# Routed tokens in 39 units of 128 rows (16 blocks of two, 7 of one) in place of 23 blocks of 256, with two raw weight buffers

## What is computed

```python
x = x + _layernorm(_L0_attn_ref(_layernorm(x), Wq, Wk, Wv, Wo, b_out))
x = x + _layernorm(_L0_ffn_ref(_layernorm(x), w_router, wg, wu, wd, sg, su, sd))

# _L0_ffn_ref: E = 8, TOPK = 2, H = 256, I = 640, NSH = 2
scores = sigmoid(xt @ w_router.T)
topk_w, topk_i = top_k(scores, 2)            # weights divided by their sum -> comb
gate = silu(einsum('th,eih->tei', xt, wg)); up = einsum('th,eih->tei', xt, wu)
out = einsum('te,teh->th', comb, einsum('tei,ehi->teh', gate * up, wd))
out = out + the same gate/up/down with sg, su, sd for the 2 shared experts, no weights
```

## Time and profile before

| what | value |
|---|---|
| median of 3 runs | 746.38 us |
| lowest, highest run | 740.99, 746.75 us |
| the profiled execution's own time | 747.06 us |
| its span, first to last instruction | 745.2 us |
| PE busy | 699.8 us, 94% of the span |
| PE weight loads busy | 556.5 us, 75% |
| DVE busy | 593.2 us, 80% |
| ACT busy | 435.8 us, 58% |
| POOL busy | 309.9 us, 42% |
| moved by DMA | 74.29 MB, mean 100 GB/s |

### The profile page before, as it was taken

The page is one execution under the profiler, slowest core; times in us unless marked ns, Lnnn a source line. Parts: engine busy times, 40 slices in busy tenths (PEclk is TensorE's granted clock), DMA queues, the critical chain, the costliest instruction groups (busy, mean ns, idle before and its releaser), DMA issues.

```text
span 745.2 us, 15380 instructions
## 1 busy us (share of the span) xinstructions
PE 699.8 (94%) x5954; PEld 556.5 (75%) x5954; DVE 593.2 (80%) x1251; ACT 435.8 (58%) x745; POOL 309.9 (42%) x445
## 2 busy tenths in 40 slices
PE   3888999999999988999999999999999999978994
PEld 2444555555555545888889999999999999867884
DVE  4999999999998884487777888888888888428885
ACT  2456766677766685442266776777777777412321
POOL 4124344444444463100264444544544531075764
PEclk9899999999999999999999999999999999998998
DMA  8000000000000000000356667667666676031211
GB/s 283 1 4 3 4 3 17 10 10 12 9 11 17 11 12 13 15 8 1 106 157 222 227 215 238 222 217 243 211 220 245 210 223 216 29 99 43 84 59 56
DMA packets 28552, 74.29 MB, mean 100 GB/s; under 512 B 4032, under 2 KB 17728, under 8 KB 28480
## 3 DMA queue, kind: packets, MB, share of 16 engines
q0 software_dynamic: 12208, 55.45, 22.9%
q1 hardware_dynamic: 15856, 17.20, 6.8%
q10 hardware_dynamic: 416, 0.66, 0.3%
HBM read 62.68 MB, written 10.22 MB: 98 GB/s over the span
## 4 chain that ended last, share of the span: by engine, by line
PE 77%; DVE 15%; issue 3%; ACT 2%; POOL 1%; DMA 1%; POOLq 0%; DVEq 0%
PE PS L438 73%; DVE NM L874 4%; DVE NM L870 3%; PE PS L449 2%; PE PS L623 1%; DVE QC L839 1%; PE PS L541 1%; DVE RR L834 1%; DVE X L1133 1%; DVE RT L846 1%; POOL RS L1221 1%; ACT PF L744 1%; DMA X<-in_x 1%; DVE KC L844 1%; DVE CTX L906 0%
## 5 line engine op out<-in xcount | busy, mean ns | idle before, releaser
L1068 DVE TENSOR_TENSOR HF<-SS,PS 128x256 f32<-128x256 f32 (+1 forms) x155 | 75.9, 490 | 95.2 <-ACT SS L787 54.1
L787 ACT ACTIVATE SS<-PS 128x256 f32<-128x256 f32 (+1 forms) x155 | 68.1, 439 | 120.1 <-PE PS L438 105.8
L438 PE MATMUL PS<-XGH,WH 128*128 128x256 f32 x460 | 129.2, 281 | 0.0
L438 PE MATMUL PS<-XGL,WH 128*128 128x256 f32 x460 | 128.9, 280 | 0.0
L438 PE MATMUL PS<-XGH,WL 128*128 128x256 f32 x460 | 128.8, 280 | 0.0
L1156 DVE TENSOR_TENSOR WL<-RAW,WH 128x768 fp32r<-128x768 f32 x125 | 119.9, 961 | 1.3 <-ACT WH L707 1.3
L438 PE MATMUL PS<-WH,HH 128*128 128x256 f32 x390 | 112.5, 289 | 7.3 <-issue 7.2
L1254 POOL TENSOR_SCALAR_AFFINE_SELECT PF<-PF 128x512 f32<-128x512 f32 x128 | 78.8, 640 | 96.8 <-ACT PF L744 96.7
L707 ACT ACTIVATE HH<-HF 128x256 fp32r<-128x256 f32 (+1 forms) x155 | 72.1, 465 | 68.9 <-DVE HF L1068 61.7
L438 PE MATMUL PS<-WL,HH 128*128 128x256 f32 x390 | 110.7, 284 | 0.0
L744 ACT ACTIVATE PF<-PS 128x1536 f32<-128x1536 f32 x64 | 92.8, 1450 | 30.6 <-PE PS L438 30.0
(11 more groups left out here) (174 smaller groups left out, 1465.7 us busy)
## 6 DMA issues: line engine op xcount, KB each, us to landing
ys<-YO SPq DMA_DIRECT2D x23, 256.0 KB
RAW<-in_wsh SPq DMA_DIRECT2D x4, 768.0 KB, 6.4
X<-in_x SPq DMA_DIRECT2D x8, 256.0 KB, 5.2
xn<-YY SPq DMA_DIRECT2D x16, 128.0 KB, 1.7
out<-X SPq DMA_DIRECT2D x16, 128.0 KB
RAW<-in_wsh SPq DMA_DIRECT2D x2, 384.0 KB, 6.2
XG<-xn,XIDX POOLq DMA_INDIRECT x46
QT<-NMT SPq DMA_DIRECT2D x32, 12.0 KB
```

The costliest lines, as they stand in the source:

```text
L438: return eng.matmul(o, l, r, start=start, stop=stop, skip_group_check=True)
L787: t = eng.activation(SS[:, i % 2, 0:n], bank(b, 0, n), ACT.Silu)
L1068: eng.tensor_tensor(HF[:, c % 2, 0:n], SS[:, c % 2, 0:n], bank(b, 512 - n, 512) if n == 256 else bank(b), ALU.mult).then_inc(free[b], 1)
```

## The change

The routed tokens lie in units of 128 slots. SUB = (4096 + 8*127) // 128 = 39 of them suffice for any routing. 16 pairs form wide blocks of 256 as before; 7 single ones are narrow blocks of 128 tokens. The number of blocks, NK, is again 23, and they run in the order W N W W N W W W N W W N W W N W W W N W W N W (W wide, N narrow), so that of UNITS. An expert whose last 256 holds at most 128 tokens puts them in a narrow one.

A narrow block has 3 chunks (2, 2 and 1 times 128 inner columns) and 121 + 20 = 141 chunks are left in all. In its `up` the tokens (XGH, XGL: 128x128) are stationary and the weights (WH, WL) move, 512 columns a matmul for a chunk of two and 256 for the last: 6 matmuls a chunk. The products HF then have tokens on the partitions, so a stage `cross` on PE transposes them (1 matmul a 128 columns) into bank 6 or 7; `hh` and `hl` of a narrow chunk read that bank and come after `cross`, one step later than for a wide chunk. `down` has 3 matmuls of 256 columns per 128 inner columns. `turn_block` has 2 transposes.

`splits()` lists at which chunk each piece is split: some 20,000 columns of matmul ahead of its use and after the last reader of its WH buffer is in the plan. In a wide block ahead of a narrow one this gives chunks with 2, 2, 1, 1 and 1 pieces; in a narrow one 1 a chunk; the five pieces of the second shared expert all stand in one chunk, the first (c = 116) of the last wide block. There are two raw buffers, RAW0 and RAW1 (the second lies where attention's small tiles were); weights are asked for two blocks ahead. The shared expert's second weights go to RAW0 and wait for the pieces of block 23, which are split in chunks 111 to 115.

`choose` 4 to 8 and 13 work on counts in 256s and in 128s: `places()` has 13 operations where 3 stood, and 5 and 13 have 1 and 2 more. The arrays over SUB shrink from 46 to 39. The weights' layout in memory is changed to match (gate and up side by side for each half of 256).

```diff
@@ -18,12 +18,20 @@
 NE = 8
 IC = 5
 TG = 4
-BLK = 256
-NK = (2 * NT * P + NE * (BLK - 1)) // BLK
-SUB = 2 * NK
+SUB = (2 * NT * P + NE * (P - 1)) // P
+WIDE = (SUB - NE + 1) // 2
+SLIM = SUB - 2 * WIDE
+UNITS = [u for _, u in sorted([((2 * k + 1) / (2 * WIDE), (2 * k, 2)) for k in range(WIDE)] +
+                              [((2 * j + 1) / (2 * SLIM), (2 * WIDE + j, 1)) for j in range(SLIM)])]
+NK = len(UNITS)
 DENSE = TG * IC
-LAST = DENSE + IC * NK
-NC = LAST + DENSE
+CHUNKS = [(0, c % IC, 1) for c in range(DENSE)]
+for k in range(NK):
+    CHUNKS += [(k + 1, m, 1) for m in range(IC)] if UNITS[k][1] == 2 else [(k + 1, 0, 2), (k + 1, 2, 2), (k + 1, 4, 1)]
+LAST = len(CHUNKS)
+CHUNKS += [(NK + 1, c % IC, 1) for c in range(DENSE)]
+NC = len(CHUNKS)
+AHEAD = 20000
...
+def wide_of(c):
+
+    return 128 * CHUNKS[c][2] if narrow(c) else 256 if DENSE <= c < LAST else 512
...
+def user(q, m):
+
+    return max(c for c in range(NC) if CHUNKS[c][0] == q and CHUNKS[c][1] <= m < CHUNKS[c][1] + CHUNKS[c][2])
+
+
+def splits():
+
+    at, first = [0], {}
+    for c in range(LAST + 1):
+        at.append(at[-1] + (4608 if not narrow(c) else 2432 * CHUNKS[c][2]))
+        for m in range(CHUNKS[c][1], CHUNKS[c][1] + CHUNKS[c][2]):
+            first.setdefault((CHUNKS[c][0], m), c)
+    out, c = {}, 0
+    for q in range(1, NK + 2):
+        for m in range(IC):
+            use = first.get((q, m), LAST + m)
+            w = max([n for n in range(min(use, LAST)) if at[n] <= at[min(use, LAST)] - AHEAD] + [DENSE - 2])
+            if q == 1:
+                w = DENSE - 2 if m < 2 else DENSE - 1
+            c = max(c, w, user(q - 2, m) + 1 if q > 1 else 0)
+            out.setdefault(c, []).append((q, m))
+    return out
...
+            if narrow(c - 1):
+                out.append(("cross", c - 1))
+                out.append(("hh", c - 1))
             out.append(("hl", c - 1))
-        q, m = sequence(c), c % IC
-        if c < DENSE:
-            pieces = {18: (0, 1), 19: (2, 3, 4)}.get(c, ())
-        else:
-            pieces = (m,) if c < LAST else ()
-        out.extend(("split", q + 1, m) for m in pieces)
-        if c < NC:
+        out.extend(("split", q, m) for q, m in pieces.get(c, ()))
+        if c < NC and not narrow(c):
             out.append(("hh", c))
...
-        elif s[0] in ("xt", "rank", "token"):
-            b = {"rank": 6, "token": 7}.get(s[0], 6 + s[1] % 2)
+        elif s[0] in ("rank", "token", "xt", "cross"):
+            b = 6 + crossed % 2
+            crossed += 1
...
-        RAW = sb("RAW", [P, 3840], F32)
+        RAW0 = sb("RAW0", [P, 3840], F32)
...
+        RAW1 = sb("RAW1", [P, 3840], F32)
+        sb("rest", [P, 320], F32)
...
+        def raw_of(q):
+
+            return 0 if q > NK else (q + 1) % 2 if q else 0
...
+                if narrow(c):
+                    o = bank(b, 0, 256 * n)
                     k6 = 0
                     for k in range(2):
-                        at = 768 * ic + 256 * m + 128 * k
-                        if block:
+                        xh = XGH[:, (q - 1) % 2, 128 * k:128 * k + 128]
+                        xl = XGL[:, (q - 1) % 2, 128 * k:128 * k + 128]
+                        wh, wl = (w[:, 768 * ic:768 * (ic + n)].rearrange("p (i c) -> p i c", c=768)[:, :, 256 * k:256 * k + 256]
+                                  for w in (hi, lo))
+                        for l, r in ((xh, wh), (xl, wh), (xh, wl)):
+                            t = mm(o.rearrange("p (i c) -> p i c", c=256), l, r, k6 == 0, k6 == 5)
+                            k6 += 1
...
+            def cross(c):
+
+                mixed(e, c)
+                b = take(("cross", c))
+                for i in range(CHUNKS[c][2]):
+                    t = eng.transpose(bank(b, 128 * i, 128 * i + 128), HF[:, c % 2, 128 * i:128 * i + 128], identf)
+                t.then_inc(full[b], 1)
...
-                        e.wait_ge(d_raw[m // 2], 16 * q)
+                        e.wait_ge(d_raw[q % 2][m // 2], 16 * ((q + q % 2) // 2))
...
-                        e.wait_ge(dn, DENSE + IC * (q - 3) + m + 1)
-                    copy(WH[q % 2][:, 768 * m:768 * m + 768], RAW[:, 768 * m:768 * m + 768]).then_inc(w_hi, 1)
+                        e.wait_ge(dn, user(q - 2, m) + 1)
+                    copy(WH[q % 2][:, 768 * m:768 * m + 768], RAW[raw_of(q)][:, 768 * m:768 * m + 768]).then_inc(w_hi, 1)
...
+                    if narrow(i):
+                        made(e, ("cross", i))
+                        copy(HH[:, i % 4, 0:n], bank(use["cross", i][0], 0, n)).then_inc(h_hi, 1)
+                    else:
+                        mixed(e, i)
+                        copy(HH[:, i % 4, 0:n], HF[:, i % 2, 0:n]).then_inc(h_hi, 1)
...
+            def places():
+
+                te = "p (t e) -> p t e"
+                c, n = use["rank", 0]
+                rank = bank(c, 0, 128).rearrange(te, e=8)
+                eng.scalar_tensor_tensor(out=CUM[:, :, :], in0=BASE[:, :, :], scalar=1.0 / 256, in1=NBK[:, :, :], op0=ALU.mult, op1=ALU.add).then_inc(lay, 1)
+                eng.tensor_scalar(BACK1[:, 0, :], NBK[:, 0, :], 256.0, None, ALU.mult, ALU.bypass)
+                eng.tensor_scalar(BACK1[:, 1, :], BASE[:, 1, :], 0.5, None, ALU.mult, ALU.bypass).then_inc(lay, 1)
+                eng.tensor_tensor(SL[:, :, :], rank, BASE[:, 0, :].unsqueeze(1).broadcast_to([P, NT, NE]), ALU.add)
+                e.wait_ge(lay, 3)
+                eng.tensor_scalar(FST[:, 0:1], CUM[:, 0, 7:8], 2.0, float(SUB - NE), ALU.mult, ALU.max).then_inc(lay, 1)
+                eng.tensor_tensor(EQ[:, :, :], rank, BACK1[:, 0, :].unsqueeze(1).broadcast_to([P, NT, NE]), ALU.is_ge).then_inc(free[c], 1)
+                eng.scalar_tensor_tensor(out=BACK1[:, 2, :], in0=CUM[:, 0, :], scalar=-256.0, in1=BACK1[:, 1, :], op0=ALU.mult, op1=ALU.add).then_inc(lay, 1)
+                e.wait_ge(lay, 4)
+                eng.tensor_scalar(FST[:, 1:2], FST[:, 0:1], 128.0, None, ALU.mult, ALU.bypass).then_inc(lay, 1)
+                e.wait_ge(lay, 6)
+                eng.tensor_scalar(CUM[:, 1, :], CUM[:, 1, :], FST[:, 0:1], None, ALU.add, ALU.bypass)
+                eng.tensor_scalar(BACK1[:, 1, :], BACK1[:, 2, :], FST[:, 1:2], None, ALU.add, ALU.bypass).then_inc(lay, 1)
+                e.wait_ge(lay, 7)
+                e.wait_ge(free[c], n)
+                eng.tensor_tensor(EQ[:, :, :], EQ[:, :, :], BACK1[:, 1, :].unsqueeze(1).broadcast_to([P, NT, NE]), ALU.mult).then_inc(lay, 1)
+                e.wait_ge(lay, 8)
+                eng.tensor_tensor(SL[:, :, :], SL[:, :, :], EQ[:, :, :], ALU.add).then_inc(lay, 1)
+                e.wait_ge(lay, 9)
+                eng.tensor_tensor(SL[:, :, :], SL[:, :, :], SG[:, 2, :].rearrange(te, e=8), ALU.mult).then_inc(rt, 1)
...
+                    eng.scalar_tensor_tensor(out=EB[:, 0, :], in0=EB[:, 0, :], scalar=NE - 0.5, in1=EB[:, 0, :], op0=ALU.is_lt, op1=ALU.mult).then_inc(rs_, 1)
                     e.wait_ge(rs_, 4)
-                    t = eng.tensor_scalar(WIDX[:, :], EB[:, :], pcol, None, ALU.add, ALU.bypass)
+                    eng.tensor_tensor(EB[:, 0, :], EB[:, 0, :], EB[:, 1, :], ALU.add).then_inc(rs_, 1)
+                    e.wait_ge(rs_, 5)
+                    eng.tensor_scalar(EB[:, 0, :], EB[:, 0, :], float(NE - 1), float(P), ALU.min, ALU.mult).then_inc(rs_, 1)
+                    e.wait_ge(rs_, 6)
+                    t = eng.tensor_scalar(WIDX[:, :], EB[:, 0, :], pcol, None, ALU.add, ALU.bypass)
...
+                    if narrow(i):
+                        c = use["cross", i][0]
+                        eng.tensor_tensor(HL[:, i % 4, 0:n], bank(c, 0, n), HH[:, i % 4, 0:n].bitcast(F32), ALU.subtract).then_inc(free[c], 1)
+                    else:
+                        eng.tensor_tensor(HL[:, i % 4, 0:n], HF[:, i % 2, 0:n], HH[:, i % 4, 0:n].bitcast(F32), ALU.subtract).then_inc(h_lo, 1)
...
             def weights(q, k):
                 lo, hi = PIECES[k]
                 e.wait_ge(w_idx, 1)
-                e.wait_ge(w_lo, IC * (q - 1) + hi)
-                eng.indirect_dma_start(RAW[:, 768 * lo:768 * hi], None, (wa, wb, wc)[k],
-                                       bass.IndirectOffsetOnAxis(ap=WIDX[:, q - 1:q], axis=0)).then_inc(d_raw[k], 16)
+                if q == 2:
+                    made(e, ("token", 0))
+                else:
+                    e.wait_ge(w_lo, IC * (q - 2 if q > 2 else 0) + hi)
+                eng.indirect_dma_start(RAW[raw_of(q)][:, 768 * lo:768 * hi], None, (wa, wb, wc)[k],
+                                       bass.IndirectOffsetOnAxis(ap=WIDX[:, q - 1:q], axis=0)).then_inc(d_raw[q % 2][k], 16)
...
+                    for k in range(3):
+                        weights(2, k)
+                elif what == "split" and 0 < i < NK - 1 and s[2] in (1, 3, 4):
+                    weights(i + 2, s[2] // 2)
...
                     if q:
-                        e.wait_ge(w_lo, IC * (q - 1) + hi)
```

(40 more changed lines are left out.)

228 lines of the change are left out of this document (122 added, 106 removed).

## The result

The changed kernel takes 721.14 us (median of 4 runs, 718.19 to 722.65), the kernel before 745.44 in as many runs beside it (740.99 to 746.75). The ratio is 0.9679, with a 95% interval of 0.9627 to 0.9732: 24.3 us, or 3.2%, faster, 2.6 us over the forecast of 718.5. The profiled execution took 720.56 with a span of 718.8.

What follows compares the result with a forecast made beforehand. PE's matmul columns were taken to bound the routed stage. From the profiled 747.06 us, minus 35.3, plus 2.8 (XGL), 3.8 (hand-over) and 0.9 (routing) gave 719.3, stated as 718.5 against the median; range 711 to 734.

Steps and rivals of the forecast that it cites:

- The gain: Routed stage: 7 narrow blocks of 6.05 us replace wide ones of 11.09, removing PE columns worth 35.3 us.
- The wait for XGL: Each narrow block: PE waits 0.4 us for XGL before the next block's first up; 2.8 us in all (0 to 7).
- The hand-over: Chunk 116, last shared expert: its late weight load, one split counted after landing, delays PE's down; loss 3.8 us (2.6 to 5.0).
- Routing: Longer places() and choose make DVE 2.7 us later at chunk 14's HF; 0.9 us lost (bounds 0 and 2.7).
- The doubled splits: Wide blocks ahead of narrow ones: DVE's two splits a chunk just fit; nothing added, upper bound 0.3 for each of 7.
- Summed up: Routed stage: DVE's total work is 195 us of 220, so PE stays the bound with 11% over it, not 18%.
- One thing stays as it is: Last stage, untouched by the change: PE's unexplained 6.90 us wait at 666 us was taken to remain.
- the second rival: Whole kernel comes out lower, at 712 us, as the hand-over is hidden or the 6.90 us pause falls away; chance 0.12.
- The first: Rival, narrow blocks: DVE paces them at 8.3 us each, 13 us more, giving 732; chance 0.15.
- The third: Rival, narrow blocks: turning gate products puts the stages in a row, 16.7 us a block, giving 786; chance 0.05.
- the fourth: Rival, routed stage: loads set the pace at 219 GB/s, needing 253 us; total 750, no change; chance 0.04.
- wrong signs: PE idle for HL or HF in narrow blocks, WH waiting for RAW, clock under 1.00 after transposes, no hand-over wait.

Runs made afterwards that it cites:

- experiment 1: Changed kernel with all 23 blocks wide and none narrow, everything else of the change kept: 739.21 us, ratio 1.0005 to the kernel before.
- experiment 7: Changed kernel with narrow blocks keeping weights stationary, 128 tokens moving and gate products not turned: 741.51 us, ratio 0.9945 to the kernel before.
- Experiment 4: Changed kernel with xt ahead of a narrow chunk's splits and bank-freeing copies (down c-2) put first: 716.45 us, ratio 0.9608 to the kernel before.
- Experiment 2: Changed kernel with the last shared expert's weights in the other raw buffer, loaded one block earlier, split one piece a chunk: 710.30 us, ratio 0.9605.
- experiment 3: Changed kernel with the second block's pieces split one a chunk, not 2, 2, 1: 714.30 us, ratio 0.9673 to the kernel before.
- experiment 6: Changed kernel with the edits of Experiment 2, experiment 3 and Experiment 4, and block 3's loads asked for one block later: 712.79 us, ratio 0.9569.

## Why the prediction was right, and where it was not

**The gain held.** A narrow block costs 6.39 us with its wait for XGL, against 6.05 + 0.4. Seven of them give 7 x (11.09 - 6.39) = 32.9 us, against 32.5. Experiments 1 and 7 show that it is their columns: without narrow blocks nothing is gained, and without the turned form 14 us of the stage are lost again. What no term of the sum had is that the 16 wide blocks became 0.11 us longer each, 1.7 us in all, at an unchanged clock; its cause is open. The 512-column matmuls advance PE by 0.233, and this was the low end of the bounds. They stand so in the timeline, followed by the `cross` pair and the turn:

```profile
599.37 0.40 PE L520 MATMUL PS<-WL,XGH 128*128 128x512 f32 x1
599.60 0.39 PE L520 MATMUL PS<-WH,XGH 128*128 128x512 f32 x1
...
600.30 0.38 PE L679 MATMUL PS<-CF,HF 128*128 128x128 f32 x2
600.51 0.60 PE L730 MATMUL PS<-CF,XG 128*128 128x128 f32 x4
600.87 0.36 PE L520 MATMUL PS<-WH,HH 128*128 128x256 f32 x1
```

Two `cross` transposes advance PE by 0.21, four of the turn by 0.36, so about 0.1 each, as taken. The granted clock of the whole group (483.34 to 512.13), with its 5 `cross` and 10 turning transposes, is 1.00. The 275 ns of the Trainium skill, "TensorE: Matmul & The Clock Gate", "Part 4: PE-mode transpose", is again a single one's duration and not its pace, and its rule that transposes don't count for the clock changed nothing in this mix.

**The wait for XGL** was 0.27 to 0.32 in all seven, against 0.4: right in place and size. Experiment 4 takes it away by moving `xt` ahead of the split, as the step's lower bound said.

**The hand-over failed in size.** The step "landed 6.9, split 7.7, HH 8.1" had the landing of the first part right (5.0 us from issue) and the rest wrong. The splits of all five pieces follow, not one, and HH waits for five; DVE's five WL in one go (4.58 us) delay HF and HL further. And a wait of that length has a tail at the lower clock. So 7.9 us instead of 3.8. Experiment 2 shows the whole of it to come from the choice of this buffer and the five splits in one chunk. The step also misread, whose landings are of the same six loads. The three at the program's start took 6.7, 8.2 and 8.6 us, and the three at the hand-over 6.1, 4.5 and, for the part of 384 KB, 3.8. So 3.8 is not a time of a 768 KB part, 6.2 is the mean of 3.8 and 8.6, and the bounds of 3.8 to 6.2 left the 8.6 out. The Trainium skill, "DMA: Bandwidth & Descriptors", section "Anatomy of one DMA — SWDGE (gpsimd) path", gives an estimated 3.8 us for 768 KB and 2.9 for 384 KB, for GpSimd's loads. The three parts here, which SP issued, took 5.0, 6.3 and 6.0, so it was not met.

**Routing failed in place.** The loss came to 1.50 us (forecast 0.9) at 349.47, not at chunk 14: DVE is 2.0 us later with the copies that free a bank (348.57 against 346.65 in the earlier trace rows, with the HF before them 0.1 earlier), and PE waits for that. `places()` itself took 2.2 us (346.36 to 348.57), as counted.

**The doubled splits** cost little in the middle (upper bound 0.3 each; of the seven blocks one shows a wait of 0.24 at 420.75), but 2.7 us at the start of the stage (experiment 3), where the copies of the dense stage's banks stand on DVE too. "Summed up" and "so it just fits" looked only at steady blocks.

**The pause was assumed to stay, and did not.** "One thing stays as it is" is the step that failed most, by 9.3 us. It was named as the second rival's case. In the profile after there is a pause of 3.4 us at another place. The stage was 10.3 us too long and the last part 9.3 too short, and that the total came within 2.6 us of the forecast is luck.

**Rivals.** The first (DVE paces the narrow blocks, 732) falls: in the group DVE is busy 24.51 of 28.79 us and PE 28.68. The second, 712, has the right mechanism in one half, the pause that falls away; its other half, a hidden hand-over, did not come, and the time is 9 us above it. The third, 786, and the fourth, 750, fall: the transposes stand in the flow of PE, and no WH waits for a gathered piece in the steady blocks, with the DMA at 253 GB/s and a share of 0.74. So of the things named as wrong signs none was seen in the narrow blocks.

## What to carry to other kernels

Where PE's columns are the limit, count them per instruction: here a matmul of 128 columns costs nearly the 256 one's time (0.112 against 0.118 us), and in `up` only the form with tokens as the stationary operand and weights moving made fewer tokens cost less. When buffers are doubled, look at where each wait for the old buffer now stands: here it kept one load waiting for the last block's own splits, and five new splits then stood in a row. And in a sum against one execution, price a pause whose cause isn't shown as a rival of its own and look whether it comes again in other runs; compare stage by stage, since two errors of 10 us may cancel, and measure an untouched block again in the changed kernel before it is used as a yardstick.

## What was not expected of the hardware

- A matmul of 128 columns advances PE by 0.112, one of 256 by 0.118, one of 512 by 0.233. The two shorter ones are the same to within 7%.
- The 90 matmuls of 256 columns in a wide block take 10.42, 10.66 or 10.77 us, in the kernel of experiment 1, the kernel before and the changed one. Every block of a kernel has the same, and the kernel before and the changed one have it in each of their three profiles. DVE is busy 9.06 and ACT 8.09 us a block in all of them, and the clock is 1.00. What makes the 3% is open.
- After waits of 2.6 and 5.6 us PE ran 3.1 and 4.8 us at the lower level (0.212 a matmul), and after the 1.8 us of experiment 2 another 3.2. After waits of 1.2 to 1.4 the matmuls kept 0.118. So a wait in a stretch of full PE costs up to 2.2 us more than it lasts.
- ACT, and at times DVE, stops for 3 to 8 us at a place that no semaphore, DMA or engine in the profile explains. All eight profiles of the second and third chip have it, none of the four of the first. That fits the 7 us by which the kernel before is faster there. Its place and length change with the kernel and the run. What makes it is open, since taking loads away from the start (experiment 6) did not remove it.
- In these rows a load's time to land goes more with what was issued beside it than with its size: at the hand-over the 384 KB part took 6.0 us where SP issued it 1.8 us after the first of three, and 3.8 in the kernel before, where it came 6.6 after the first.
